# A vision tower's image recurrence: two products a block that nothing reads on TensorE, and rows weighed ahead of the sum on VectorE

## What is computed

```
# x: 16 images (the scan's axis) x 3137 tokens x 64 channels, after the residual of the memory
x = x + y_tok * (prb * kept)               # the experts' rows, gathered and weighed
xp = einsum(layernorm(x), W_ih) + b_ih + b_hh
def step(h, xp_t):
    h_new = tanh(xp_t + h @ W_hh.T)
    return h_new, h_new
_, hiddens = scan(step, 0, xp)             # over the images: token by token, independent
x = x + hiddens                            # kept as h3
y = layernorm(x)                           # input of the slice attention
```

## Time and profile before

| | |
|---|---|
| median of 3 runs | 3720.48 us (3715.47 to 3722.12) |
| the profiled execution | 3721.05 us, its span 3719.4 us |
| PE, PEld, DVE, ACT, POOL busy in the span | 3073.6, 1790.7, 2503.1, 2118.4, 2197.5 us |
| first to last gather of stage D | 1968.2 to 2636.3 us (starts) |
| 2060 to 2640 us: granted TensorE clock | 0.79 |
| 2060 to 2640 us: PE, DVE, ACT, POOL busy | 391.38, 191.17, 328.49, 320.60 us |

### The profile page before, as it was taken

One profiled execution on the slowest core, in us unless ns is written; L12 is line 12 of the kernel. 1 busy time (PEld: TensorE's weight loads), 2 busy tenths in 40 slices (PEclk: granted clock), 3 DMA queues, 4 the chain that ended last, 5 costly groups with the idle time before them and its releaser, 6 DMA issues. The chain is left out here.

```text
span 3719.4 us, 71632 instructions
## 1 busy us (share of the span) xinstructions
PE 3073.6 (83%) x26456; PEld 1790.7 (48%) x26456; DVE 2503.1 (67%) x3488; ACT 2118.4 (57%) x3070; POOL 2197.5 (59%) x1391
## 2 busy tenths in 40 slices
PE   8999999698889888729993666676778999999997
PEld 5777777445555555413441222222224555555555
DVE  7888888678888888617771333333367787777873
ACT  5666767487777777404442655555744455554552
POOL 7777777315888888750005555555166676666761
PEclk9999999899999999859996888787889999999999
DMA  1111111102221122115542333333211222121222
GB/s 41 41 37 42 39 39 42 59 25 57 65 64 55 48 56 56 38 56 166 152 144 56 95 91 98 92 99 94 95 46 35 58 59 57 53 55 52 63 54 49
DMA packets 240543, 243.84 MB, mean 66 GB/s; under 512 B 79965, under 2 KB 166982, under 8 KB 239818
## 3 DMA queue, kind: packets, MB, share of 16 engines
q1 hardware_dynamic: 206106, 195.39, 17.7%
q0 software_dynamic: 25600, 26.01, 3.0%
q10 hardware_dynamic: 8496, 17.87, 1.3%
HBM read 125.29 MB, written 113.87 MB: 64 GB/s over the span
## 5 line engine op out<-in xcount | busy, mean ns | idle before, releaser
L1762 POOL DMA_INDIRECT D_row<-yb,P_gi x400 | 382.4, 956 | 601.5 <-DMA D_prob<-keepp 314.8
L635 POOL DMA_INDIRECT xb<-B_yt,P_gi x400 | 519.1, 1298 | 122.3 <-issue 113.7
L2373 POOL TENSOR_TENSOR E_w<-E_w,E_rs 128x1024 f32<-128x1024 f32 x200 | 380.3, 1902 | 306.6 <-DVE E_rs L2296 306.6
L191 POOL TENSOR_TENSOR A_kmask<-A_ksb,A_pack_a 128x3584 f32<-128x3584 f32 x56 | 356.4, 6364 | 152.3 <-ACT A_ksb L338 152.3
L2367 POOL TENSOR_TENSOR E_hs<-E_w 128x512 f32<-128x512 f32 x200 | 255.1, 1276 | 77.1 <-ACT E_w L2255 77.1
L2255 ACT ACTIVATE E_w<-E_w 128x1024 f32<-128x1024 f32 x200 | 211.4, 1057 | 132.5 <-DVE E_w L2288 129.8
L2280 DVE TENSOR_REDUCE E_mx<-E_lg 128x16 f32<-128x1024 f32 x188 | 223.6, 1189 | 73.9 <-PE E_lg L2104 73.3
L1930 DVE TENSOR_TENSOR D_h<-D_x,D_hid 128x512 f32<-128x512 f32 (+1 forms) x56 | 35.6, 636 | 342.9 <-ACT D_hid L1869 267.7
L420 DVE COPY A_vbd<-A_v 128x512 f32<-128x512 f32 x392 | 248.8, 680 | 15.0 <-PE A_v L278 14.9
L2104 PE MATMUL E_lg<-S_wxs,E_ya 64*128 64x512 f32 x752 | 223.8, 670 | 14.6 <-DMA E_ya<-y 8.5
L2251 ACT ACTIVATE E_ob<-E_o 128x128 f32<-128x128 f32 (+1 forms) x187 | 51.8, 277 | 317.6 <-PE E_o L2146 295.6
(11 more groups left out here) (325 smaller groups left out, 7391.2 us busy)
## 6 DMA issues: line engine op xcount, KB each, us to landing
R_xs<-xb SPq DMA_DIRECT2D x57, 256.0 KB, 2.7
yb<-R_ys SPq DMA_DIRECT2D x57, 256.0 KB, 2.0
B_x<-h SPq DMA_DIRECT2D x25, 512.0 KB
h<-B_hh SPq DMA_DIRECT2D x25, 512.0 KB
A_xg<-in_xw SPq DMA_DIRECT2D x56, 224.0 KB, 2.9
h<-A_res ACTq DMA_DIRECT2D x56, 224.0 KB, 2.0
D_hx<-h SPq DMA_DIRECT2D x48, 256.0 KB
h<-D_h SPq DMA_DIRECT2D x48, 256.0 KB
```

Source lines behind the costliest of these rows:

```text
L191: nc.gpsimd.tensor_tensor(kmask[i % 2][:], bc(ksb[i % 2][:].unsqueeze(2), [128, J, H, Q]), bc(head_of_row[:].unsqueeze(1).unsqueeze(3), [1 ...
L635: pool.indirect_dma_start(out=xb, out_offset=bass.IndirectOffsetOnAxis(ap=routed.gi[0:k, c, b:b + 1], axis=0), in_=yt[c % LT][0:k, D * row ...
L1762: pool.indirect_dma_start(out=row[n % LR][:, k, b], out_offset=None, in_=yb, in_offset=bass.IndirectOffsetOnAxis(ap=idx[:, c, i:i + 1], ax ...
L2373: TT(w3, w3, bc(rs[g % 3][:].unsqueeze(2), [128, 2 * SH, G]), ALU.mult).then_inc(w_done, 1)
```

## The change

On PE two products are added for each block, both by `busy`: the centring matrix times the packed constants, 512 columns (128 for a narrow block), into the buffer of `pc` or `px` which the next real product writes with `start=True`. Nothing reads them. The first stands ahead of `center_in` and waits until the buffer of `pc` is free, no longer for `x`; the second stands ahead of `inputs` and waits until the buffer of `px` is free, no longer for `y`. `turn_y` moves from the start of the turn to behind `center_in`, and `variance` from the end to ahead of `variance_out`. The waits for the one `pt` follow: `turn_rows(n)` waits for `yk` of block n-6, `turn_y(n)` for `x` of block n+5.

On DVE `weigh` moves to the head of the turn and `add_hidden` behind it, one turn later than before (block t-3 in turn t, before t-2); `tokens` moves behind `add_experts`, since its transposes come later.

```diff
--- before.py
+++ after.py
@@ -1772,14 +1772,19 @@
                 def turn_rows(n):
                     pe.wait_ge(sc_done, n + 1)
                     after(pe, x_done, n)
-                    after(pe, yk_done, min(n - 4, N))
+                    after(pe, yk_done, n - 5)
                     for k in range(len(tiles(n))):
                         last = turn(pt[:, TILE * k:TILE * k + TILE], scaled[:, k].rearrange("p b d -> p (b d)"), ident[:])
                     last.then_inc(tr_done, 1)
 
+                def busy(bank, n):
+
+                    mm(bank[:, 0:wide(n)], center[:], pack[:, 0:wide(n)], start=True, stop=True, skip_group_check=True)
+
                 def center_in(n):
+                    after(pe, y_done, n - 1)
+                    busy(pc[n % 2], n)
                     pe.wait_ge(x_done, n + 1)
-                    after(pe, y_done, n - 1)
                     mm(pc[n % 2][:, 0:wide(n)], center[:], x[n % 3][:, 0:wide(n)], start=True, stop=True).then_inc(cen_done, 1)
 
                 def variance(n):
@@ -1788,8 +1793,9 @@
                     mm(pv[:, 0:wide(n)], mean[:], sq[:, 0:wide(n)], start=True, stop=True).then_inc(var_done, 1)
 
                 def inputs(n):
+                    after(pe, tb_done, n - 1)
+                    busy(px[n % 2], n)
                     pe.wait_ge(y_done, n + 1)
-                    after(pe, tb_done, n - 1)
                     mm(px[n % 2][:, 0:wide(n)], wih[:], y[:, 0:wide(n)], start=True, stop=n < J,
                        skip_group_check=True).then_inc(ih_done, 1)
 
@@ -1816,21 +1822,21 @@
 
                 def turn_y(n):
                     pe.wait_ge(yo_done, n + 1)
-                    after(pe, x_done, min(n + 5, N))
+                    after(pe, x_done, min(n + 6, N))
                     for k in range(len(tiles(n))):
                         last = turn(pt[:, TILE * k:TILE * k + TILE], yo[n % 2][:, TILE * k:TILE * k + TILE], ident[:])
                     last.then_inc(ty_done, 1)
 
                 for t in range(N + 5):
-                    at(turn_y, t - 5)
                     at(turn_rows, t)
                     at(center_in, t)
+                    at(turn_y, t - 5)
                     at(inputs, t - 1)
                     at(center_out, t - 3)
                     at(first_hidden, t - 1)
                     at(second_hidden, t - 2)
+                    at(variance, t)
                     at(variance_out, t - 3)
-                    at(variance, t)
 
             @block.scalar
             def _(act):
@@ -1947,12 +1953,12 @@
                     V.tensor_copy(yk[n % 2][:, 0:k].rearrange("p c d -> p (c d)"), pt[:, 0:wide(n)]).then_inc(yk_done, 1)
 
                 for t in range(N + 5):
+                    at(weigh, t)
+                    at(add_hidden, t - 3)
+                    at(add_experts, t)
                     at(tokens, t - 5)
-                    at(weigh, t)
-                    at(add_experts, t)
                     at(normed_in, t - 1)
                     at(normed_out, t - 4)
-                    at(add_hidden, t - 2)
 
 
 def slice_attention(nc, a, h3, y4, y4t, out, fixed):
```

## The result

The changed kernel takes 3747.86 us (median of 19 runs, 3727.81 to 3761.34) against 3723.51 for the kernel before on the same chip (19 runs, 3706.3 to 3738.33): ratio 1.0063, 95% interval 1.005 to 1.0077. It is 24 us slower. The forecast was 3690, faster; its range of 3650 to 3770 holds the measured time, but only for the sake of its slow rivals. The profiled execution is the slowest of the 19, 3761.34 us, its span 3759.7.

The account below looks back on a forecast made before the run. Bound: a loop of waits in the image recurrence, no engine full, clock 0.79. From 3721 us: middle turns -35, fast and slow turns 0, after the last gather -4, start +7, together -32, said as 3690; range 3650 to 3770.

Parts of the forecast that it names:

- slow rivals: The two rival forecasts of a slower kernel: fillers counted against PE (3756 us, chance 0.24), longer runs of gathers (3770, 0.12).
- What bounds the kernel: Image recurrence, 1968 to 2700 us: a loop of waits, no engine full, clock 0.79, PE's completions late during gather runs.
- About 12 us into such a run: Where late completions were said to begin in a run of sixteen POOL gathers; they end 2 to 3 us after it.
- DVE order: Weighing ahead of the sum with the recurrent state: one wait replaces another, 4 us at most, left out of the sum.
- That wait goes: DVE's sum with the recurrent state would no longer wait for the second tanh; 243.8 us idle to fall under 60.
- The two fillers: Two unread PE products a block, in PE's longest gaps: zero cost in a cold turn, middle turns from 10.65 to 8.9 us.
- Slow turns 0: The twenty of 46 turns taking 13 to 18.6 us would neither gain nor lose: late completions last as long as POOL runs.
- Middle turns, -35: Twenty of 46 turns, 9.4 to 11.7 us each, would go from 10.65 to 8.9 us in the mean: -35 us.
- The fillers use up what PE may have outstanding: Rival, chance 0.24: lateness follows PE's instruction count in a gather run, fillers bring it sooner: +35 us, 3756.
- Longer runs: Rival, chance 0.12: earlier weighing lets POOL gather 24 times in a row, three turns taking 44 us: +50, 3770 us.
- The pool sets the cycle: Rival, chance 0.15: gathers fix the cycle's length, so a faster first turn gives nothing back: no change, 3720 us.
- After the last gather: Once POOL's gathers end, two or three turns at the low clock (0.87) would speed up: -4 us.

## Why the prediction was wrong, point by point

- **What bounds the kernel.** Right: a loop of waits with late completions beside long runs of gathers. The gathers cause them; without them the stage shrinks by some 200 us. "About 12 us into such a run" was read from one run; the stage has 10.7 to 20.8.
- **DVE order.** "That wait goes" was wrong. The sum of block t-3 in turn t needs the second tanh of the same block, which is still the last thing in ACT's turn before; the wait fell from 288.6 to 178.1 us, not to under 60. It costs little in a warm turn and holds the next centring in a late one. The new wait before the copy of the tokens came as forecast, and that the order by itself is worth nothing here was right (ratio 1.0000), though the old wait stayed beside the new one. What it does to the clock I missed.
- **The two fillers.** The step that failed is the term "Slow turns 0". That the second filler "is hidden, warm (0.86) and nearly so cold (1.71)" was worked out in the waits of a warm turn, and I priced slow turns at 0 since "the late completions last as long as POOL runs". They do, but how far PE has come by then sets what is left behind the run. In place of 0 the runs show 2.9 us in each of 20 cycles in the old order, where the output centring then always came behind the run, and 5.0 us in each of the five runs of 24 in the changed kernel. Slow turns went from 20 of 15.4 us to 22 of 17.0.
- **Middle turns, -35.** They went as forecast (20 to 4) and gained nothing: a faster turn outside a late stretch only let the next run of gathers meet its late stretch at an earlier point of the work, or grow to 24. The gain in a class of turns was added up as if the others stood still.
- **The rivals.** "The fillers use up what PE may have outstanding" had the sign, and its time of 3756 is within 10 us of the measured one. That is luck in part: it put them at 35 us, where they cost 57 alone and 24 with the long runs of the new order. Its basis is open. For it: with fillers lateness begins sooner, and behind nearly the same count, 60, in fourteen runs of seventeen. Against it: 40 to 85 before, and 81 in the changed kernel's long runs. The Trainium skill (TensorE: Matmul & The Clock Gate, table at its top, row "Engine queue depth") states a queue of 64; by it the count should have been alike in all kernels, and it is in one only. "Longer runs" came (five of 24), cost nothing without fillers and more with them. "The pool sets the cycle" is half the truth: gathers set the cycle, and what PE has not got through in their late stretches is added to it.
- **After the last gather.** Right: 0.94 of the clock.

## What to carry to other kernels

Sort the turns of a loop before pricing an edit, and ask for each class whether the wait that is to hide it exists there; a filler that is free in a warm turn can cost where completions come late, by pushing the next step behind the run that makes them late. Where a row says "issue", look at what ended just before it on the other engines: a wait that was to go may still be there. Read how a wait marked "remote" lines up with another engine's runs: the remedy for late completions of TensorE was on GpSimd, 0.2 us of idle work behind each indirect gather. And run a remedy of that kind on several chips, since on one of five nothing seemed to be late.

## What the hardware showed that I had not expected

- Completions of TensorE are late, by 8.1 us in the row above, while GpSimd issues indirect gathers 1.25 or 1.33 us apart for more than some 9 us (in the stage's first run, with PE starting up, only after 33). They are not late with 1.44 us (400 in a row), not in runs of eight with a pause between, not with plain transfers 0.53 us apart (300 in a row). They flow again 1 to 3 us behind the last gather. Why, no run here tells.
- Four chips ran the kernel before in 3716 to 3739 us and a fifth, in its one sitting, in 3527.
